# Two passes of a graph kernel on one core: narrower products of ones on TensorE in the last turns of both passes

## The chip, the core and the metric

One core of a Trainium2 chip runs the kernel. The metric is the device time of one execution in microseconds (us), lower is better. Engines are named as in the profile: PE is TensorE's matrix products, PEld its weight loads, DVE is VectorE, ACT is ScalarE, POOL is GpSimd, SP is SyncE, which here only issues transfers. A "q" behind an engine's name (SPq, ACTq) is its queue of issued transfers.

## What is computed

There are 100,000 nodes with 64 features each and 50,000 edges (src, dst) with 32 attributes each. Cut to what matters:

```python
h = relu(layernorm(x))                       # first layer
s, m, c = segment_sum(attr, src), segment_max(attr, src), count(src)
f = concat([s, m, s / max(c, 1), u[0]])      # 97 features of a node
x = x + relu(f @ W1 + b1) @ W2 + b2
h = relu(layernorm(x))                       # second layer
agg = segment_sum(h[src], dst)
x = x + relu(agg @ W.T + b)
```

The `h` of the first layer is not used by it. A node with no edge gets a constant row in either layer, a node with edges gets its own; so the work is done by edge, in sorted order, and the rows are then spread over the nodes.

## The kernel before

**Blocks and passes.** The edges are sorted by src first (up to about 226 us, not touched here). Then come two passes, each over 98 blocks (`BLOCKS`) of 512 edges (`BLK`). Pass 1 (side 0, about 226 to 730 us) computes the rows of the first layer and adds them to x, giving the table `node_table`. Pass 2 (side 1, about 731 us to the end) gathers rows of `node_table` for the source node of each edge, normalizes them, multiplies them by W, and adds the result to the table on the way to the output. Edge rows go out to memory as records (`records<-rec`, line 694), one store for a block. Of them, windows are loaded back: for each step of 1,024 nodes, eight windows of 112 records (`win<-records`). In pass 1 SP issues six of the eight (line 388) and ACT two (line 667); in pass 2 each issues four.

**Expansion.** The helper `expand(side, m)` on PE turns the windows of node step m into 1,024 node rows. Eight products (lines 1378 and 1379), each of a 128 by 128 one-hot matrix with 64 columns of a window, fill one bank of PSUM with 512 columns. In fp32 each product shows in the profile as two weight loads and two products, so an expansion is 16 records. What it needs: its one-hot matrices (`hot_ok`, made by DVE at line 1095: tile `oneh` in pass 1, `shared` in pass 2), and a free bank (`added`, counted by DVE after it has added a finished expansion to the table's rows, lines 1114, 1116 and, for the last twelve steps of pass 2, 1105). The banks are `p_t` and `p_u` in pass 1 and `p_t`, `p_u`, `p_z` in turn in pass 2.

**Products of ones.** The helper `stream(bank, width)` at line 1384 multiplies a matrix of ones with `width` columns of ones into a bank that the following expansion overwrites. Nothing reads the result. In `expand` it stands between the wait for the bank and the wait for the one-hots, over 512 columns (line 1376); this is the product ahead. In pass 2 a second one, over 256 columns, stands behind each expansion but the last (lines 1423 to 1425), with a wait for the next bank; this is the product behind. Each shows in the profile as two records of PE at line 1384.

**Order by hand.** Each engine runs a list of turns n, each turn working on blocks and steps of different age. In pass 1 PE does in turn n the transposes of block n+1, the expansion of step n-6 (`SRC_EXP`), the second layer of block n-1 (line 1367) and the first of block n (line 1360). Turns 98 to 103 have no new block. In pass 2 PE does in turn n the expansion of step n-9 (`DST_EXP`), the product behind, the multiplication by W of block n-2 (`conv`, line 1416) and the transposes of block n (`turn_h`, line 1408). Turns 98 to 106 have no new block: they expand steps 89 to 97, and the first two also have a `conv`. DVE in turn n of pass 2 reads the keys of windows n-8 (line 1085), takes the moments of block n, makes the one-hots of step n-8 (line 1095), normalizes block n (line 1182) and adds step n-10. SP and ACT load the windows of step n-6.

**Rings.** There are two buffers of one-hots: in pass 2 line 1093 makes the one-hots of step m wait until expansion m-2 is done. There are four buffers of windows: in pass 2 the loads for step m wait until expansion m-4 is done (lines 386 and 665), and until the records of block m+1 are stored. In pass 1 SP has the wait for the expansion only for the last step, ACT for the last six. ACT's queue also holds, ahead of its window loads in each turn, the copy of a block into a record and its store (lines 683 to 694). SP's queue holds, behind its window loads, the loads of the table's rows and the stores of finished ones (lines 394, 398, 424).

Of the kernel before, what the change touches and what calls it, by code (L numbers as in the profile page):

```python
# [26 lines left out]
BLK = BT * P  # L27
BLOCKS = -(-E // BLK)
# [32 lines left out]
SRC_REC, SRC_WIN, SRC_HOT, SRC_EXP, SRC_ADD, SRC_PUT = 1, 3, 5, 6, 7, 9  # L61
DST_TAKE, DST_CONV, DST_REC, DST_WIN, DST_HOT, DST_EXP, DST_ADD, DST_PUT = 1, 2, 3, 6, 8, 9, 10, 12
# [7 lines left out]
def valid(n):  # L70

    return 0 <= n < BLOCKS


def build(nc, x, src, dst, edge_attr, u, W1, b1, W2, b2, W, b, src_keys, dst_keys, src_cols, dst_cols, dst_lines, out):
# [5 lines left out]
    with ExitStack() as ctx:  # L81
# [258 lines left out]
        def _(sp):  # L340
# [35 lines left out]
            def windows(side, m):  # L376

                g = BLOCKS * side + m
                starts = start_row[side][0:1, PER * m:PER * m + SP_LOADS[side]]
                _, at = nc.values_load_multi_w_load_instructions(starts, engines=[mybir.EngineType.SP], min_val=0, max_val=E * ROW,  # L380
                                                                 skip_runtime_bounds_check_because="each start is a count of rows, lowered to its limit on the chip")
                for n in range(AHEAD + 1) if m == 0 else [min(m + AHEAD, BLOCKS - 1)]:
                    stored = BLOCKS * side + n
                    sp.wait_ge(rec_out[stored % RRING], 16 * (stored // RRING + 1))
                if side == 1 or m == BLOCKS - 1:
                    sp.wait_ge(expanded, g - WRING + 1)
                for q in range(SP_LOADS[side]):
                    sp.dma_start(win[g % WRING][0:WP, q, :].bitcast(U8), window_rows(side, at[q])).then_inc(win_in[g % WRING], 16)
# [220 lines left out]
        def _(act):  # L609
# [45 lines left out]
            def upper_windows(side, m):  # L655

                g = BLOCKS * side + m
                starts = start_row[side][0:1, PER * m + SP_LOADS[side]:PER * (m + 1)]
                _, at = nc.values_load_multi_w_load_instructions(starts, engines=[mybir.EngineType.Activation], min_val=0, max_val=E * ROW,
                                                                 skip_runtime_bounds_check_because="each start is a count of rows, lowered to its limit on the chip")  # L660
                for n in range(AHEAD + 1) if m == 0 else [min(m + AHEAD, BLOCKS - 1)]:
                    stored = BLOCKS * side + n
                    act.wait_ge(rec_out[stored % RRING], 16 * (stored // RRING + 1))
                if side == 1 and m < WRING or m >= BLOCKS - DST_WIN:
                    act.wait_ge(expanded, g - WRING + 1)
                for q in range(PER - SP_LOADS[side]):
                    s.dma_start(win[g % WRING][0:WP, SP_LOADS[side] + q, :].bitcast(U8), window_rows(side, at[q])).then_inc(win_in[g % WRING], 16)  # L667
# [615 lines left out]
        def _(pe):  # L1283
# [15 lines left out]
            def sum_starts(side, nth):  # L1299

                pe.wait_ge(s_above, nth)
                for h, row in enumerate(p_s[side]):
                    for k in range(SPAN):
                        last = mm(row[0:1, 0:400], in_group[:, k:k + 1], above[:, k, 400 * h:400 * (h + 1)],
                                  start=k == 0, stop=k == SPAN - 1)
                last.then_inc(s_base, 1)
# [43 lines left out]
            def turn_attr(n):  # L1350
                if n == 1:
                    pe.wait_ge(s_col, 2)
                pe.wait_ge(scaled, n + 1)
                for t in range(BT):
                    last = tr(p_g[n % 2][0:2 * FE, t::BT], xa[n % XRING][:, t, :], ident[:, :])
                last.then_inc(turned, 1)

            def layer1(n):
                pe.wait_ge(feats_ok, n + 1)
                mm(p_z[n % 2][:, :], w1_s[:, :], feats[n % 2][:, :], start=True, stop=True).then_inc(z_ok, 1)  # L1360

            def layer2(n):
                pe.wait_ge(hid_ok, n + 1)
                if n >= 1:
                    pe.wait_ge(copied, n)
                for t in range(BT):
                    last = mm(p_m[0][:, D * t:D * (t + 1)], hid[n % 2][:, P * t:P * (t + 1)], w2_s[:, :], start=True, stop=True)  # L1367
                last.then_inc(m_ok, 1)

            def expand(side, m):  # L1370
                k = BLOCKS * side + m
                ring = p_e[side]
                to = ring[m % len(ring)]
                if side == 1 or m >= 2:
                    pe.wait_ge(added, max(k - len(ring) + 1, BLOCKS * side))
                stream(to, BLK)
                pe.wait_ge(hot_ok, k + 1)
                for s in range(PER):
                    last = mm(to[:, D * s:D * (s + 1)], hots[side][m % HRING][:, s, :], win[k % WRING][:, s, 0:D], start=True, stop=True)  # L1379
                last.then_inc(expanded, 1)  # L1380

            def stream(bank, width):

                mm(bank[:, 0:width], one[:, :], one[:, :].unsqueeze(1).to_broadcast([P, width // P, P]), start=True, stop=True)  # L1384

            turn_attr(0)
            for n in range(BLOCKS + SRC_EXP):
                if valid(n + 1):
                    turn_attr(n + 1)
                if n == 2:  # L1390
                    sum_starts(0, 2)
                if valid(n - SRC_EXP):
                    expand(0, n - SRC_EXP)
                if valid(n - 1):
                    layer2(n - 1)
                if n == 15:
                    pe.wait_ge(s_wrong, 1)
                    mm(p_m[1][0:1, 0:1], wrong1[:, 0:1], one[:, 0:1], start=True, stop=True).then_inc(s_wsum, 1)
                if valid(n):
                    layer1(n)  # L1400

            pe.wait_ge(s_fast, 1)
            with pe.If(pe.value_load(fast[0:1, 0:1], min_val=0, max_val=1)):

                def turn_h(n):
                    pe.wait_ge(h_ok, n + 1)
                    for h in range(2):
                        last = tr(p_g[n % 2][:, P * h:P * (h + 1)], hn[n % 2][:, 2 * h:2 * h + 2, :].rearrange("p t d -> p (t d)"), ident[:, :])  # L1408
                    last.then_inc(ht_ok, 1)

                def conv(n):
                    k = BLOCKS + n
                    pe.wait_ge(hts_ok, n + 1)
                    pe.wait_ge(copied, max(k - 1, BLOCKS))
                    for h in range(2):
                        last = mm(p_d[1][n % 2][:, P * h:P * (h + 1)], agg[n % 2][:, P * h:P * (h + 1)], wd[:, :, :].rearrange("p t d -> p (t d)"),
                                  start=True, stop=True)
                    last.then_inc(m_ok, 1)

                for n in range(BLOCKS + DST_EXP):  # L1420
                    if valid(n - DST_EXP):
                        expand(1, n - DST_EXP)
                    if valid(n - DST_EXP) and valid(n - DST_EXP + 1):
                        pe.wait_ge(added, max(BLOCKS + n - DST_EXP + 1 - len(p_e[1]) + 1, BLOCKS))
                        stream(p_e[1][(n - DST_EXP + 1) % len(p_e[1])], BLK // 2)
                    if valid(n - DST_CONV):
                        conv(n - DST_CONV)
                    if valid(n):
                        turn_h(n)
# [61 lines left out]
```

## Time and profile before

| | |
|---|---|
| median of 3 runs | 1256.63 us |
| lowest and highest of them | 1252.74, 1262.65 us |
| the profiled execution's own time | 1261.67 us |
| its span, first to last instruction | 1259.8 us |
| mean granted clock of TensorE | 0.888 of 2.4 GHz |

The profile is of one execution, 5.0 us above the median of the three runs. A line of a timeline or of the chain gives a start and a length in us, the engine, the line of the kernel and the operation; in brackets stands how long the engine had been idle before it and what ended that. In a table of windows the granted clock (PEclk) is 1.00 at 2.4 GHz and 0.50 at 1.2 GHz.

### The profile page before, as it was taken

How to read it: one execution, taken by the hardware profiler on the slowest of the kernel's cores; microseconds unless marked ns; L12 is line 12 of the kernel's file. 1: busy time of each engine (PE TensorE's matmuls, PEld its weight loads, DVE VectorE, ACT ScalarE, POOL GpSimd, SP SyncE). 2: the span in 40 equal slices, each digit the busy share in tenths (PEclk: the TensorE clock that was granted, in tenths of full speed). 3: DMA queues.
4: the chain of work that ended last, by engine and by line, in shares of the span. 5: the costliest groups of instructions: out<-in, count | busy, mean ns of one | idle time of the engine just before them, and what ended most of it. 6: DMA issues, size and time to landing. Idle time of an engine off the chain costs nothing.

```text
span 1259.8 us, 20767 instructions
## 1 busy us (share of the span) xinstructions
PE 960.6 (76%) x5818; PEld 758.0 (60%) x5818; DVE 1030.1 (82%) x2727; ACT 280.1 (22%) x681; POOL 758.0 (60%) x821
## 2 busy tenths in 40 slices
PE   0131027979999999999999823879889788888888
PEld 0010014757777777777777613767767677677777
DVE  8888887899999999999999624777777777777774
ACT  1441042212222222222222101112112112111110
POOL 3000046667777777777776067777777777777750
PEclk9995556889999999999999955898999989988899
DMA  2000012767899888888888654777788778777775
GB/s 65 0 0 0 0 53 68 175 161 206 236 232 240 234 226 219 241 220 236 230 222 240 164 173 98 180 201 203 210 222 207 202 198 210 210 208 201 203 186 156
DMA packets 317563, 218.51 MB, mean 173 GB/s; under 512 B 223428, under 2 KB 255140, under 8 KB 317444
## 3 DMA queue, kind: packets, MB, share of 16 engines
q1 hardware_dynamic: 182100, 135.41, 38.7%
q10 hardware_dynamic: 110256, 62.42, 18.8%
q0 software_dynamic: 25088, 19.32, 8.6%
q8 instruction: 47, 0.77, 0.3%
q14 instruction: 72, 0.59, 0.1%
HBM read 137.51 MB, written 79.45 MB: 172 GB/s over the span
## 4 chain that ended last, share of the span: by engine, by line
DVE 36%; POOL 20%; DMA 13%; PE 11%; issue 10%; ACTq 5%; ACT 2%; SPq 0%; POOLq 0%; DVEq 0%
POOL xa L559 11%; POOL xa L540 9%; DMA xa<-node_table,gi 8%; DMA win<-records 5%; DVE feats L1074 4%; DVE feats L1072 4%; ACTq L667 3%; DVE oneh L1095 3%; DVE dout L1114 2%; PE p_m L1367 2%; DVE kb L920 2%; DVE ka L920 2%; DVE shared L1095 2%; DVE ka L921 2%; DVE kb L921 2%
## 5 line engine op out<-in xcount | busy, mean ns | idle before, releaser
L540 POOL DMA_INDIRECT xa<-in_edge_attr_dram,gi x392 | 375.2, 957 | 252.3 <-issue 115.4
L559 POOL DMA_INDIRECT xa<-node_table,gi x392 | 369.9, 944 | 158.7 <-issue 105.8
L677 ACT ACTIVATE hid<-p_z,bias_z 128x512 f32<-128x512 f32 x98 | 113.4, 1157 | 249.2 <-issue 230.0
L1408 PE MATMUL p_g<-ident,hn 128*128 128x128 f32 x196 | 46.6, 325 | 106.9 <-DVE hn L1182 106.5
L1074 DVE TENSOR_TENSOR_SCAN feats<-c_rows,feats,p_g 32x512 f32<-32x512 f32 x97 | 123.3, 1271 | 1.4
L1095 DVE SCALAR_TENSOR_TENSOR shared<-p_m,node_of 112x1024 f32<-112x1024 f32 x98 | 117.1, 1195 | 6.8 <-PE p_z L1379 3.4
L1072 DVE TENSOR_TENSOR_SCAN feats<-c_rows,feats,p_g 64x512 f32<-64x512 f32 x97 | 122.5, 1263 | 0.1
L1367 PE MATMUL p_m<-w_s,hid 128*128 128x64 f32 x784 | 109.3, 284 | 15.8 <-ACT hid L677 15.4
L730 ACT ACTIVATE sd<-mv,eps_t 128x4 f32<-128x4 f32 x98 | 29.1, 297 | 413.2 <-DVE mv L1173 350.4
L1095 DVE SCALAR_TENSOR_TENSOR oneh<-p_m,node_of 112x1024 f32<-112x1024 f32 x98 | 119.3, 1217 | 0.2
L1360 PE MATMUL p_z<-feats,w_s 96*128 96x512 f32 x196 | 112.4, 657 | 6.2 <-DVE feats L1074 6.2
L1168 DVE BATCH_NORM_STATS2 stat<-xa 128x6 f32<-128x64 f32 x392 | 58.7, 212 | 67.6 <-DMA xa<-node_table,gi 63.9
L1379 PEld LDWEIGHTS p_u<-win,oneh 128*128 128x128 f32 x784 | 97.1, 195 | 26.9 <-issue 22.5
L1384 PE MATMUL p_t<-one 128*128 128x256 f32 (+1 forms) x228 | 112.5, 578 | 0.0
L1379 PEld LDWEIGHTS p_t<-win,oneh 128*128 128x128 f32 x784 | 96.4, 194 | 25.5 <-issue 24.1
L1384 PE MATMUL p_u<-one 128*128 128x512 f32 x230 | 110.7, 566 | 0.0
L1367 PEld LDWEIGHTS p_m<-w_s,hid 128*128 128x128 f32 x784 | 97.6, 196 | 21.5 <-ACT hid L677 19.9
L1379 PE MATMUL p_u<-win,oneh 128*128 128x64 f32 x784 | 94.9, 275 | 2.2 <-DVE oneh L1095 2.2
L1408 PEld LDWEIGHTS p_g<-ident,hn 128*128 128x128 f32 x196 | 25.0, 159 | 117.8 <-DVE hn L1182 116.9
L1085 DVE COPY p_m<-win 112x8 f32<-112x8 f32 x196 | 32.8, 167 | 75.9 <-DMA win<-records 75.7
L1379 PE MATMUL p_t<-win,oneh 128*128 128x64 f32 x784 | 93.9, 273 | 0.5 <-DVE oneh L1095 0.5
L1182 DVE SCALAR_TENSOR_TENSOR hn<-xa,mv,p_m 128x64 f32<-128x64 f32 x392 | 83.9, 276 | 3.5
(253 smaller groups left out, 1539.3 us busy)
## 6 DMA issues: line engine op xcount, KB each, us to landing
win<-records SPq DMA_DIRECT2D x980, 28.9 KB
records<-rec ACTq DMA_DIRECT2D x196, 132.0 KB
din<-in_x_dram SPq DMA_DIRECT2D x49, 512.0 KB
node_table<-dout SPq DMA_DIRECT2D x49, 512.0 KB, 3.6
din<-node_table SPq DMA_DIRECT2D x43, 512.0 KB
out_dram<-dout SPq DMA_DIRECT2D x43, 512.0 KB
c_rows<-rows_src ACTq DMA_DIRECT2D x141, 128.0 KB
win<-records ACTq DMA_DIRECT2D x588, 28.9 KB
```

The costliest lines, as they stand in the source:

```text
L540: g.indirect_dma_start(out=xa[n % XRING][:, t, 0:FE], out_offset=None, in_=edge_attr, in_offset=bass.IndirectOffsetOnAxis(ap=gi[0][:, BT * ...
L559: g.indirect_dma_start(out=xa[k % XRING][:, t, :], out_offset=None, in_=T, in_offset=bass.IndirectOffsetOnAxis(ap=gi[1][:, BT * n + t:BT * ...
L677: s.activation(hid[n % 2][:, :].rearrange("p (t n) -> p n t", n=P), p_z[n % 2][:, :].rearrange("p (n t) -> p n t", t=BT), ACT.Relu, bias=b ...
L1072: v.tensor_tensor_scan(f[0:64, :], c[0:64, at:at + BLK], p_g[n % 2][0:64, :], first[0:64], ALU.mult, ALU.add)
L1074: v.tensor_tensor_scan(f[64:96, :], c[64:96, at:at + BLK], p_g[n % 2][0:32, :], first[64:96], ALU.min, ALU.max).then_inc(feats_ok, 1)
L1095: v.scalar_tensor_tensor(hots[side][m % HRING][0:WP, :, :], key_at(k).unsqueeze(2).to_broadcast([WP, PER, UNIT]), -float(STEP * m), node_o ...
L1182: last = v.scalar_tensor_tensor(hn[n % 2][:, t, :], xa[(BLOCKS + n) % XRING][:, t, :], mv[n % 2][:, t, 0:1], up[:, t:t + 1].to_broadcast([ ...
L1360: mm(p_z[n % 2][:, :], w1_s[:, :], feats[n % 2][:, :], start=True, stop=True).then_inc(z_ok, 1)
L1367: last = mm(p_m[0][:, D * t:D * (t + 1)], hid[n % 2][:, P * t:P * (t + 1)], w2_s[:, :], start=True, stop=True)
L1379: last = mm(to[:, D * s:D * (s + 1)], hots[side][m % HRING][:, s, :], win[k % WRING][:, s, 0:D], start=True, stop=True)
L1384: mm(bank[:, 0:width], one[:, :], one[:, :].unsqueeze(1).to_broadcast([P, width // P, P]), start=True, stop=True)
L1408: last = tr(p_g[n % 2][:, P * h:P * (h + 1)], hn[n % 2][:, 2 * h:2 * h + 2, :].rearrange("p t d -> p (t d)"), ident[:, :])
```

## The change

In turns that have no new block, the product ahead of an expansion covers 128 columns in place of 512, and in pass 2 the one behind it is left out, with its wait. In pass 1 this is so in turns 99 to 103 (steps 93 to 97; turn 98 keeps 512). In pass 2 it is so in turns 98 to 106 (steps 89 to 97); the product behind is issued in turns 9 to 97 and no longer in turns 98 to 105.

```diff
-            def expand(side, m):
+            def expand(side, m, ones=BLK):
...
-                stream(to, BLK)
+                stream(to, ones)
...
-                    expand(0, n - SRC_EXP)
+                    expand(0, n - SRC_EXP, BLK if n <= BLOCKS else BLK // 4)
...
-                        expand(1, n - DST_EXP)
-                    if valid(n - DST_EXP) and valid(n - DST_EXP + 1):
+                        expand(1, n - DST_EXP, BLK if valid(n) else BLK // 4)
+                    if valid(n - DST_EXP) and valid(n):
                         pe.wait_ge(added, max(BLOCKS + n - DST_EXP + 1 - len(p_e[1]) + 1, BLOCKS))
                         stream(p_e[1][(n - DST_EXP + 1) % len(p_e[1])], BLK // 2)
```

## Rows read from the trace of the kernel before

**Rows 1.** The page: busy time by engine, and the chain's shares

```profile
PE 960.6 (76%) x5818; PEld 758.0 (60%) x5818; DVE 1030.1 (82%) x2727; ACT 280.1 (22%) x681; POOL 758.0 (60%) x821
...
DVE 36%; POOL 20%; DMA 13%; PE 11%; issue 10%; ACTq 5%; ACT 2%; SPq 0%; POOLq 0%; DVEq 0%
```

**Rows 2.** Chain of waits, last turns of pass 2: start us, us, what

```profile
1225.72 0.67 PE p_g L1408 x2
1226.39 1.71 PE p_z L1384 x2
1228.10 2.32 PE p_z L1379 x16
1230.42 0.49 PE p_t L1384 x2
1230.91 0.44 PE p_m L1416 x4
1231.35 0.86 PE p_t L1384 x2
1232.21 1.73 PE p_t L1379 x16
...
1252.85 1.34 PE p_u L1384 x4
1254.19 1.75 PE p_u L1379 x16
```

**Rows 3.** Table of windows: length, busy of PE, PEld, DVE, ACT, POOL, PEclk, DMA, GB/s

```profile
1178.50:1188.20 9.70, 9.63 (x32) 7.39 (x32) 7.53 (x34) 1.96 (x8) 7.26 (x9) 0.50 0.75 199
...
1223.80:1225.70 1.90, 0.12 (x2) 0.00 (x0) 1.86 (x7) 0.73 (x4) 0.00 (x0) 1.00 0.32 55
1225.90:1229.20 3.30, 3.30 (x11) 2.27 (x11) 2.29 (x5) 0.74 (x3) 0.00 (x0) 0.50 0.42 102
1229.30:1255.90 26.60, 26.60 (x178) 22.25 (x177) 14.36 (x22) 0.93 (x4) 0.00 (x0) 1.00 0.61 169
708.00:720.00 12.00, 11.33 (x77) 8.72 (x75) 7.01 (x11) 1.48 (x2) 0.00 (x0) 1.00 0.59 146
...
724.00:727.00 3.00, 2.43 (x13) 2.24 (x11) 1.23 (x2) 0.00 (x0) 0.00 (x0) 0.51 1.01 391
```

**Rows 4.** Chain of waits, last turns of pass 1

```profile
720.05 1.79 DMA win<-records
...
722.07 1.23 DVE oneh L1095
...
723.35 3.09 PE p_u L1379 x16
726.46 0.70 DVE dout L1114
```

**Rows 5.** Chain of waits, a stretch of pass 2 at the low clock

```profile
1180.96 3.31 PE p_u L1379 x16
1184.27 0.96 PE p_z L1384 x2
1185.23 0.85 PE p_m L1416 x4
```

**Rows 6.** Timeline, last turns of pass 1, PE and DVE

```profile
718.37 2.00 PE L1379 MATMUL p_t<-win,oneh 128*128 128x64 f32 x16 [0.51 <-DVE oneh L1095]
...
724.86 0.69 DVE L1114 TENSOR_TENSOR dout<-p_t,din 128x512 f32<-128x512 f32 x1 [1.56 <-DMA din<-in_x_dram]
```

**Rows 7.** Timeline, last turns of pass 2, windows' loads and keys

```profile
1236.32 9.91 ACTq L667 DMA_DIRECT2D win<-records  x16
...
1240.68 1.73 SPq L388 DMA_DIRECT2D win<-records  x4
...
1246.82 0.17 DVE L1085 COPY p_m<-win 112x8 f32<-112x8 f32 x1 [1.34 <-DMA win<-records]
```

**Rows 8.** Table of windows, two us in which PE waited for DVE

```profile
1202.00:1204.00 2.00, 0.93 (x6) 0.51 (x5) 1.84 (x8) 0.06 (x1) 1.41 (x2) 1.00 0.94 335
```

## The prediction

> **What bounds the kernel now.** I read the page first, then the chain of waits at the end of either pass, then tables of windows with the granted clock, then the timeline. Over the whole span PE is busy for 960.6 us and has 11% of the chain; DVE has 36% [rows 1]. That mean says little here, since the change touches 14 of the 196 expansions, all of them where a pass runs out.
>
> At the end of pass 2 the picture is another one. From 1225.72 us, when the last transposes start, to 1255.94 us, when the last expansion is done, the chain is PE alone [rows 2], and from 1229.3 to 1255.9 PE is busy for all of 26.60 us, DVE for 14.36 [rows 3]. The reader should see the pattern of a turn: products of ones for 1.34 us (0.49 behind and 0.86 ahead), then an expansion for 1.73, together 3.08 us. So 44% of the path is work whose result nobody reads.
>
> At the end of pass 1 no product of ones is on the chain. It ends with a load of windows that lands at 721.84, one-hots until 723.30, the last expansion from 723.35, and DVE's add from 726.46 [rows 4].
>
> **The change in pass 2.** It removes 9 times 384 columns ahead and 8 products of 256 columns behind. By TensorE's granted clock, all of this costs one of two prices.
>
> At 2.4 GHz (PEclk 1.00): 512 columns take 0.86 us [rows 2], so 128 take 0.22, and the `conv` products confirm it: four records of 128 columns in 0.44 us. A turn's own PE work falls from 3.08 us to 0.22 + 1.73 + about 0.05 = 2.0 us.
>
> At 1.2 GHz (PEclk 0.50): an expansion takes 3.31 us, the product of 256 columns behind it 0.96, `conv` 0.85 [rows 5], and 512 columns take 1.71 [rows 2]. So 128 columns take 0.43. The first record behind an expansion costs 0.11 more (0.96 against half of 1.71). A turn is then 0.43 + 0.11 + 3.31 = 3.85 us, which is more than the 3.08 of today. An expansion at the low clock loses 1.58 us, and the removed products give back 1.12 at most at the high one (0.64 + 0.49). The sign hangs on which level the last nine turns get.
>
> What do the rows show of the level? PE stands idle from about 1223.9 to 1225.7, waiting for the last block's normalization, and the clock then is 0.50 from 1225.9 to 1229.2 [rows 3]. Today that low stretch is filled with the transposes, a product of 512 columns, and some of an expansion, and the clock is back at 1.00 from 1229.3. After the change only 128 columns stand there, and from then on nearly all of PE's time is expansions. The nearest rows to such a mix at the low level are from 1178.5 to 1188.2: PE busy for 9.63 of 9.70 us with an expansion, products of ones and `conv`, and the clock at 0.50 for all of it [rows 3]; it rose only as a `conv`, transposes and a whole product of 512 columns had followed each other. Expansions with their many weight loads did not bring it up there; 512 columns in a row did, there and at 1229. The change takes away just these. I therefore take the low price for all nine turns.
>
> The sum, from 1226.39 where the product ahead of step 89 starts: nine expansions, 9 x 3.31 = 29.79; the first product ahead, 0.43; two gaps with `conv`, each 0.96 + 0.43 = 1.39, so 2.78; six gaps of 0.54, so 3.24. Together 36.24 us, up to 1262.63. Today it is 29.55 us, up to 1255.94 [rows 2]. Pass 2 ends 6.7 us later.
>
> All else stays hidden: DVE needs 0.17 + 1.23 + 0.69 = 2.1 us a turn [rows 4, 6, 7], and the windows' loads need less than four turns of 3.85 (below). The wait that goes with the product behind is for a bank that the next expansion waits for anyway, so it costs and gives nothing; between 0 and 0.05 us a turn.
>
> In sentences of its own, the Trainium skill: the page "TensorE: Matmul & The Clock Gate", section "Why this matters for your kernels", says that keeping TensorE continuously busy brings it to full clock. By that rule the tail, in which products still follow each other without a gap, would be back at 1.00 soon after 1229, and the result would be that of the third case below. This trace doesn't bear it out: 9.63 us busy of 9.70, at 0.50 throughout [rows 3].
>
> **The change in pass 1.** It removes 5 times 384 columns, 5 x 0.64 = 3.2 us of PE's time at the high clock, from a stretch in which PE is busy for 11.33 of 12.00 us [rows 3] but in which the last expansions wait for one-hots: step 96 starts at 718.37, released by DVE after an idle 0.51 us [rows 6], and step 97 is released by DVE at 723.35. Nothing of the gain is on the path: 0. What can be lost is the clock. If it falls before 720, step 96 takes 3.31 and a wait of about 0.4 behind step 95 instead of 2.0, and ends near 722.2. Its add by DVE waits for a load until 724.86 anyway [rows 6], and step 97's one-hots don't wait for it. Step 97 takes 3.09 now, most of it at the low level (0.51 from 724.0 [rows 3]); wholly at the low level it takes 3.31. So pass 1 costs +0.2 us; bounds: 0 and, if each of five expansions were on the path at 1.58 us more, 7.9. I take 0.2, since the chain's order (load, one-hots, expansion) doesn't lead through earlier expansions.
>
> Both parts: +6.9 us. On the profiled execution's own time, 1261.67 (span 1259.8 and 1.9 around it), that makes 1268.6. That execution is 5.0 above the median of the three runs, so on the median, 1256.6, I forecast 1263.5 us.
>
> **The rivals.** *Upper level at first, then lower.* Idle time does not always bring the clock down: from 1202 to 1204 PE was busy for only 0.93 of 2.00 us and the clock stayed 1.00 [rows 8]. So in some executions step 89 starts at 1.00. Then PE has 2.0 us of work a turn and must wait for windows: the load of step 96's windows may start when expansion 92 is done at 1240.54; SP starts it at 1240.68, it has landed at 1246.82 [rows 7], and 0.28 later, with 1.23 for the one-hots and 1.75 for the expansion, the ring of four is closed: 9.5 us for four steps, 2.4 us a turn, and ACT's 9.91 us for 16 loads say 2.5. PE idles a fifth of each turn, more in the first ones, where ACT still has copies and stores ahead of its loads, and the clock may fall midway. Four turns at 2.4 save 4 x 0.68 = 2.7, five at 3.85 lose 3.8: together with pass 1 +1.3, 1258 us.
>
> *Upper level all the way.* Then eight turns of 2.4 to 2.5 us, 19.6, follow on step 89's end, which comes at about 1228.4. The end is 1248.0 instead of 1255.94; with the ACT queue's first turns about 7 us are gained: 1250 us. For it speaks that PE at 1.95 of 2.4 us is busier than in 1202 to 1204; against it, the idle stretch of 1223.9 to 1225.7 with so little behind it.
>
> *Slower beyond what can be told.* The clock falls in pass 1's last turns as well, and there the expansions become the path. It decides from the point where an expansion at the low level with its product, 3.85 us, is longer than the time between one-hots, 3.4 to 5 us now (718.37 to 723.35). Then up to 7.9 us come on top: 1271 us. Against it speaks the wait of 0.51 us that is there to be used, and that loads set the last step.
>
> That the change doesn't do what it says I exclude: each narrower product is certain to be issued as written.
>
> **How the numbers follow.** Forecast (low level in pass 2's tail, 1263.5): 0.57. Mixed (1258): 0.22. Upper level throughout (1250): 0.13. Pass 1 on the path too (1271): 0.06. The rest, 0.02, is for a gain in which even the ring of windows is faster. Runs of the kernel before spread by 5 us to either side, so each case has some 3 us of its own for a median. The forecast's own range is 1259 to 1268; the range takes in the mixed case down to twice its spread, 1258 - 6 = 1252, and on the other side a part of pass 1's bound, 1263.5 + 6.5 = 1270; the case at 1250 is mostly left out. A measurement of this kernel can tell about 1%, 12.6 us, from no change. No case but the last one reaches it, and part of the forecast's upper end: slower 0.08. Faster by it would need more than the ring of windows gives: 0.02. Within 1%: 0.90.
>
> **What would show it.** Right: in pass 2's tail PE without gaps, PEclk 0.50 from about 1226 to the end, expansions of 3.31 us, turns of 3.85; the last add near 1262.6 of the same start; pass 1's end later by no more than 0.4. Wrong: PEclk 1.00 behind 1230 with keys (line 1085) waiting for the windows' loads in every turn, turns of 2.4 us; or PE waiting at line 1379 for one-hots; or in pass 1 step 97's expansion released by PE's own queue and not by DVE.

## The result and the profile after

| | before | changed |
|---|---|---|
| median | 1257.90 us (20 runs) | 1263.47 us (20 runs) |
| lowest and highest | 1252.74, 1269.87 | 1257.20, 1274.43 |
| the profiled execution | 1261.67 | 1257.20 |
| mean granted clock in it | 0.888 | 0.873 |

The changed kernel takes 1.0037 times the time of the one before (95% interval 1.0021 to 1.0054). On 1257.9 us that is 4.7 us more, between 2.6 and 6.8. The loss is below the 1% of the forecast's bound, but with 20 runs a side it is clear of the noise. The three runs shown ahead of the prediction had a median of 1256.63, the twenty have 1257.90.

The profiled execution of the changed kernel was its fastest of twenty. Whole spans therefore can't be compared, nor the shares of the chain. They moved a great deal by themselves: DVE 36% and POOL 20% before [rows 1], and now

```profile
DVE 29%; POOL 25%; PE 15%; DMA 12%; issue 11%; ACTq 5%; ACT 2%; DVEq 0%; POOLq 0%; SPq 0%
```

Nor do PE's 15%, after 11%, come from the two ends of the passes that the change touches: there expansions and products of ones have some 30 us of the chain after the change, and some 33 before. DVE and POOL changed places in the middle of the passes, where the code is the same. What can be compared is a *tail*, from one instruction to another at the end of a pass. I use two. The tail of pass 2 goes from the start of the last transposes (line 1408) to the start of DVE's last add (line 1105): 1225.72 to 1255.96, 30.24 us, in the profile before. The tail of pass 1 goes from the start of the last block's second layer (line 1367) to the start of the last add (line 1114): 707.48 to 726.46, 18.98 us.

After the change, the timeline of PE and DVE in the last turns of pass 2, with the idle time before an instruction in brackets:

```profile
1221.39 0.44 PE L1408 MATMUL p_g<-ident,hn 128*128 128x128 f32 x2 [1.45 <-DVE hn L1182]
...
1221.89 1.90 PE L1379 MATMUL p_z<-win,shared 128*128 128x64 f32 x16
...
1229.77 2.00 PE L1379 MATMUL p_z<-win,shared 128*128 128x64 f32 x16 [0.79 <-DVE shared L1095]
...
1231.18 0.17 DVE L1085 COPY p_m<-win 112x8 f32<-112x8 f32 x1 [0.88 <-DMA win<-records]
...
1232.74 3.60 PE L1379 MATMUL p_t<-win,shared 128*128 128x64 f32 x16 [0.70 <-DVE shared L1095]
```

its chain of waits from there,

```profile
1232.74 3.60 PE p_t L1379 x16
1236.34 0.53 PE p_u L1384 x2
1236.88 3.31 PE p_u L1379 x16
...
1248.40 3.32 PE p_u L1379 x16
...
1251.74 0.69 DVE sign_out L1105
```

and a table of windows, with the busy time of PE, PEld, DVE, ACT and POOL, then the granted clock:

```profile
1219.70:1221.30 1.60, 0.24 (x3) 0.05 (x1) 1.56 (x7) 0.51 (x3) 0.00 (x0) 1.00 0.27 54
1221.40:1232.80 11.40, 9.91 (x85) 9.53 (x85) 7.95 (x13) 1.67 (x7) 0.00 (x0) 1.00 0.70 176
1233.00:1251.70 18.70, 18.70 (x88) 18.51 (x87) 8.96 (x14) 0.00 (x0) 0.00 (x0) 0.50 0.52 151
698.00:710.50 12.50, 9.62 (x71) 8.14 (x69) 6.82 (x12) 2.61 (x4) 0.00 (x0) 1.00 0.79 208
710.70:722.40 11.70, 11.36 (x52) 11.17 (x52) 4.95 (x8) 0.01 (x1) 0.00 (x0) 0.50 0.62 170
```

The reader should see a tail in two parts. Up to 1232.8 the clock is 1.00 and PE has time to spare: 9.91 us busy of 11.40, with steps 92 and 93 waiting for windows' keys and the one-hots made of them. From about 1233 the clock is 0.50, PE is busy without a gap, and a turn takes 0.53 + 3.31 = 3.84 us where it was 3.08 [rows 2]. What four steps gain at 2.4 GHz, five at 1.2 GHz lose: the tail is 1221.39 to 1251.74, 30.35 us against 30.24. In pass 1 the chain after the change reads

```profile
709.74 1.23 DVE oneh L1095
710.98 0.04 issue
711.02 3.68 PE p_u L1379 x16
714.70 0.53 PE p_t L1384 x2
715.23 3.31 PE p_t L1379 x16
718.54 0.53 PE p_u L1384 x2
719.07 3.32 PE p_u L1379 x16
722.41 0.70 DVE dout L1114
```

where before it went through a load and step 97's one-hots [rows 4]. The last three expansions run at the low level one behind the other and are the path; the first of them started late, after PE had waited 3.00 us for its one-hots. The tail is 702.18 to 722.41, 20.23 us against 18.98.

### The profile page after: what moved, and what is told of

The parts are those of the page before. It is cut to its first block, busy times and chain, and to the rows that moved or that the text cites. A ratio compares the mean times of both kernels' runs of the same rounds, so it can differ in the third digit from the quotient of the medians.

```text
span 1255.4 us, 20735 instructions
## 1 busy us (share of the span) xinstructions
PE 964.8 (77%) x5802; PEld 771.3 (61%) x5802; DVE 1031.4 (82%) x2727; ACT 280.5 (22%) x681; POOL 757.6 (60%) x821
## 4 chain that ended last, share of the span: by engine, by line
DVE 29%; POOL 25%; PE 15%; DMA 12%; issue 11%; ACTq 5%; ACT 2%; DVEq 0%; POOLq 0%; SPq 0%
POOL xa L540 15%; POOL xa L559 9%; DMA xa<-node_table,gi 8%; DMA win<-records 4%; ACTq L667 3%; PE p_u L1379 3%; PE p_t L1379 3%; DVE feats L1074 3%; DVE feats L1072 2%; DVE kb L920 2%; DVE ka L920 2%; DVE oneh L1095 2%; PE p_m L1367 2%; DVE shared L1095 2%; DVE ka L921 2%
## 5 line engine op out<-in xcount | busy, mean ns | idle before, releaser
L1384 PE MATMUL p_u<-one 128*128 128x512 f32 (+1 forms) x224 | 110.0, 576 | 0.0
L1384 PE MATMUL p_t<-one 128*128 128x256 f32 (+2 forms) x222 | 108.9, 575 | 0.0
L1379 PEld LDWEIGHTS p_t<-win,shared 128*128 128x128 f32 x528 | 79.1, 230 | 18.9 <-issue 17.2
```

## The experiments

Diffs are against the kernel before, unless said, and cut to the lines that matter: where a call has a width, `expand` and `stream(to, ones)` are as in the change. All of them change only products of ones, which nothing reads, and the waits that go with them. Each kernel was profiled once, so a tail is one execution's and says nothing of how often it comes; each was timed 8 to 12 times beside the kernel before on the same chip. The last column is the granted clock of TensorE over the whole kernel, as the mean of these timed executions, and behind the slash the same for the kernel before beside them. One execution's clock scatters by some 0.0045 around the mean, so a mean of twelve is good to about 0.0013. For the change itself it is the mean of its twenty.

| run | ratio to before, 95% | tail, pass 1 | tail, pass 2 | PE idle before the last transposes | clock in the tail of pass 2 | clock, all timed executions |
|---|---|---|---|---|---|---|
| before | 1 | 18.98 | 30.24 | 1.81 | low for 3.4 us, then high | 0.886 to 0.889 |
| the change | 1.0037, 1.0021 to 1.0054 | 20.23 | 30.35 | 1.45 | high, low from step 93 | 0.874 / not on record |
| pass 1's part | 1.0009, 0.9984 to 1.0033 | 19.31 | 28.57 | 0 | high | 0.883 / 0.888 |
| pass 2's part | 1.0020, 0.9993 to 1.0047 | 16.91 | 36.43 | 2.04 | low from step 89 | 0.878 / 0.888 |
| behind left out | 0.9991, 0.9960 to 1.0022 | 17.06 | 26.37 | 0.82 | high | 0.886 / 0.888 |
| 128 ahead, 256 behind | 0.9998, 0.9971 to 1.0025 | 17.77 | 28.92 | 1.54 | low 3.4 us, high, low at the end | 0.884 / 0.888 |
| the change again | 1.0018, 0.9989 to 1.0047 | 18.16 | 30.86 | 0.35 | high, low within step 92 | 0.873 / 0.886 |
| turn 98 full | 1.0007, 0.9979 to 1.0035 | 20.13 | 30.84 | 0 | high, low within step 93 | 0.875 / 0.886 |
| no products | 1.0006, 0.9976 to 1.0036 | 19.29 | 32.48 | 2.05 | low from step 89 | 0.876 / 0.886 |
| 256 ahead | 1.0019, 0.9990 to 1.0047 | 18.34 | 30.43 | 1.91 | low 10 us, high, low at the end | 0.881 / 0.886 |
| change, turn 97 filled | 1.0034, 1.0013 to 1.0054 | 20.02 | 29.61 | 0 | high, low within step 93 | 0.874 / 0.887 |
| behind out, turn 97 filled | 0.9978, 0.9957 to 1.0000 | 16.80 | 25.88 | 0 | high | 0.887 / 0.887 |
| behind left out, again | 0.9976, 0.9953 to 0.9999 | 19.22 | 26.67 | 0.94 | high | 0.886 / 0.887 |
| behind out, filled, again | 1.0005, 0.9980 to 1.0029 | 18.00 | 25.21 | 0 | high | 0.888 / 0.889 |

The last column tells what one profile each cannot: over all timed executions the clock is lower by 0.013 with the change (its second timing), by 0.005 with pass 1's part and by 0.010 with pass 2's part, and in the four timings that keep 512 columns ahead and leave out only the product behind it differs from the kernel before by some 0.001 or less, which is noise.

**Pass 1's part alone.**

```diff
-                    expand(0, n - SRC_EXP)
+                    expand(0, n - SRC_EXP, BLK if n <= BLOCKS else BLK // 4)
```

> Only pass 1's part of the change: 128 columns ahead of steps 93 to 97, pass 2 as before. Theory (pass 1's last step is set by its windows' loads, the products of ones are beside the path, and the expansions at the low clock cost a little): +0.2 to +1.5 us against the kernel before. Rival (the five expansions become the path at 3.31 in place of 1.73 us): +6 to +8 us. Second rival (the removed 3.2 us of products were on the path): -1 to -3 us.

The ratio says +1.1 us, with an interval from 2.0 less to 4.2 more. That leaves out the 6 to 8 us of the first rival. It does not leave out the second rival's -1 to -3 us; against that one speaks the profile, in whose chain of the last turns no product of ones stands. The chain still ends in the windows' load and the one-hots, but the last expansion runs at 1.2 GHz for all of its length:

```profile
719.15 1.78 DMA win<-records
...
721.17 1.24 DVE oneh L1095
...
722.45 3.69 PE p_u L1379 x16
726.16 0.70 DVE dout L1114
```

Over all profiles the tail of pass 1 has a mean of 19.6 us in the five with the narrow products (18.2 to 20.2) and of 18.0 us in the nine with 512 columns (16.8 to 19.3). The ranges overlap; the means differ by 1.5 us. The low level is not the narrow products' alone: it came in the last steps of all five tails with them, but also in four of the nine with 512 columns (the profile before, no products in pass 2, and the second timings of the two kernels with nothing behind), where PE had waited 1.27 to 2.16 us for one-hots and an expansion took up to 3.68 us.

**Pass 2's part alone.**

```diff
-                        expand(1, n - DST_EXP)
-                    if valid(n - DST_EXP) and valid(n - DST_EXP + 1):
+                        expand(1, n - DST_EXP, BLK if valid(n) else BLK // 4)
+                    if valid(n - DST_EXP) and valid(n):
```

> Only pass 2's part: 128 columns ahead of steps 89 to 97 and nothing behind steps 89 to 96. Theory (the clock of the tail decides): executions differ. With the low level from step 89 on +6.7 us, with the high level for the first half about +0 to +1.5 us; median +4 to +6 us; expansions of 3.31 us at the end of the profile. Rival (pass 2's part gains as its work at 2.4 GHz says, and pass 1 is what makes the change slower): -6 to -8 us.

This execution shows the forecast's case from end to end. The table of windows:

```profile
1226.00:1228.10 2.10, 0.14 (x2) 0.00 (x0) 2.06 (x8) 0.93 (x4) 0.00 (x0) 1.00 0.34 54
1228.80:1264.50 35.70, 35.70 (x169) 35.58 (x167) 16.04 (x25) 1.68 (x7) 0.00 (x0) 0.50 0.47 133
```

and the chain of waits:

```profile
1228.84 3.31 PE p_z L1379 x16
1232.14 0.96 PE p_m L1416 x4
1233.10 0.43 PE p_t L1384 x2
1233.53 3.31 PE p_t L1379 x16
...
1241.53 0.53 PE p_z L1384 x2
1242.06 3.31 PE p_z L1379 x16
...
1264.61 0.69 DVE sign_out L1105
```

PE is busy for 35.70 of 35.70 us, and for all of them at 1.2 GHz: expansions of 3.31 us, gaps of 1.39 with `conv` and of 0.53 without. From the first product ahead at 1228.62 to the last expansion's end it is 35.96 us; the forecast's sum said 36.24. The tail of 36.43 us is 6.2 longer than that of the profile before. The rival, that pass 2 gains and pass 1 loses, falls: the twelve timed executions give +2.5 us, between -0.9 and +5.9. That is also less than the +4 to +6 that I expected of them; by the medians, 1264.48 against 1260.11, it is 4.4. The profiled execution, 1270.10 us, is the second longest of the twelve and not the typical one.

**The product behind left out, alone.** Run twice.

```diff
-                    if valid(n - DST_EXP) and valid(n - DST_EXP + 1):
+                    if valid(n - DST_EXP) and valid(n):
```

> Only the product behind is left out in turns 98 to 105; the one ahead keeps its 512 columns in both passes. Theory (the product ahead alone holds the clock up once it is up, as it does in pass 1, where there is none behind): turns of 0.86 + 0.05 + 1.73 = 2.65 us in place of 3.08, eight of them, -3 to -4 us. Rival (any product taken out of the tail brings the low clock): a turn is 1.71 + 0.11 + 3.31 = 5.1 us, up to +16 us.

> The run with only the product behind left out once more, for a second profiled execution and more times: tail of pass 2 26 to 29 us (28 if the level falls in turn 97 and 512 columns bring it back), level high in the last eight turns; total -1 to -4 us against the kernel before. Rival (the first profile was lucky, the level falls midway in others): a tail over 31 us.

Half of the change's idea is sound. With 512 columns ahead of each expansion the clock stays up, and the work that is taken out comes off the tail:

```profile
1225.00:1252.00 27.00, 25.65 (x172) 20.31 (x172) 17.71 (x30) 1.67 (x7) 0.00 (x0) 1.00 0.64 174
```

The tails are 26.37 and 26.67 us, against 30.24 and 28.57 in the two profiles that have before's pass 2. The last steps wait for windows' keys instead. The rival (any product taken out brings the low clock) falls. The totals moved by 1.1 us the first time, less than the 3 to 4 expected and within the noise, and by 3.0 us the second.

**128 ahead, 256 behind.**

```diff
-                        expand(1, n - DST_EXP)
+                        expand(1, n - DST_EXP, BLK if valid(n) else BLK // 4)
```

> Pass 2 only: 128 columns ahead of steps 89 to 97, the 256 behind kept. Columns of ones in a turn: 384, against 768 before, 128 in the change and 512 in the run with the behind left out. Theory (fewer columns in the tail leave the clock low after PE's wait in turn 97, and 384 are between): at the high level 2.45 us a turn, -4 to -5 us; at the low level 0.96 + 0.43 + 3.31 = 4.7 us a turn, +14 us; I expect the median between -4 and +4 us, with more spread than before. Rival (it is a wait for the bank that goes with the product behind, not the clock, that matters): same sign and size as the run with the behind left out, mirrored.

The low level was entered behind the wait in turn 97, 2.1 us after the last transposes had started, left 3.4 us later, and entered again at 1247.2, in time for the last two steps. Tail 28.92 us, ratio 0.9998: between the change and the run without the product behind, as the theory has it. The wait for the bank is still there in this kernel and makes no difference that can be seen: at the high level a turn takes 2.44 us (1232.47 to 1234.91), and its products alone ask for 0.22 + 1.73 + 0.49.

**The change again, and with a full turn 98.** The first is the change's code with one empty line less, so its lines are one lower. The second, against the changed kernel:

```diff
-                        expand(1, n - DST_EXP, BLK if valid(n) else BLK // 4)
+                        expand(1, n - DST_EXP, BLK if n <= BLOCKS else BLK // 4)
```

> The change itself once more, for another profiled execution. Tail of pass 2 = from the start of the last transposes to DVE's last add; 30.2 us in the profile before, 30.4 in the first one after, 36.3 in that of pass 2's part alone. Theory (the granted clock decides each execution's tail): the tail is near 36 us if the level is low from step 89 on, 30 to 34 if it falls later, and each expansion in it takes either 1.7 or 3.3 us. Rival (the windows' loads decide it): tails alike, 29 to 31 us, whatever the level. Pass 1, from the last block's second layer to the last add: 19.5 to 21 us against 17 to 19 before.

> The change, but turn 98 keeps its 512 columns ahead of step 89 (nothing behind it). Theory: where the level falls in turn 97, the 512 columns can bring it back, and then it falls later or not at all; tail of pass 2 29 to 33 us, never 36. Rival (the low level is entered again whatever stands in turn 98, for the eight turns with 128 columns are too thin): 35 to 36.5 us in this profile too.

The change's second profile was like the first: high until 1240.1, then low for 21.7 us, tail 30.86 us. It lay within both expectations, so the level and not the tail's length is what speaks here: its expansions take 1.7 us up to 1239 and 3.3 after. Its tail of pass 1, 18.16 us, was shorter than the 19.5 to 21 that I expected. The run with the full turn 98 is inconclusive on its question. Its last transposes started without a wait, the level did not fall there, and the 512 columns had nothing to bring back; the level fell at 1246.5, after PE had waited 1.80 us for one-hots. The run with 256 columns ahead, below, keeps 512 in turn 98 too and does answer it.

**No products of ones in the tail of pass 2.**

```diff
-                stream(to, BLK)
+                if ones:
+                    stream(to, ones)
...
-                        expand(1, n - DST_EXP)
-                    if valid(n - DST_EXP) and valid(n - DST_EXP + 1):
+                        expand(1, n - DST_EXP, BLK if valid(n) else 0)
+                    if valid(n - DST_EXP) and valid(n):
```

> Pass 2 only: no product of ones at all in turns 98 to 106; pass 1 as before. Theory: nothing is left that could lift the level, so all but perhaps the first steps run at 1.2 GHz, but a turn is then the bare expansion, 16 x 0.2133 = 3.41 us, and the two conv at 0.85: from the last transposes 0.4 + 9 x 3.4 + 1.7 = 32.9 us to the last expansion's end, so a tail near 33 us, +2.5 to +3 us against before and 3 to 4 less than the change at the low level. Rival (the products of ones cost nothing by themselves, and the windows' loads or DVE set the tail): 30 us or less. Second rival (the 128 columns of the change are of use to the clock): longer than the change's 36.

```profile
1231.20:1262.80 31.60, 31.60 (x149) 31.48 (x148) 16.18 (x24) 1.68 (x7) 0.00 (x0) 0.50 0.54 150
```

The tail is 32.48 us, 0.5 below the sum. Both rivals fall: at the low level the 128 columns of the change only cost, 36.43 - 32.48, some 3.9 us for nine of them.

**256 ahead, nothing behind.**

```diff
-                        expand(1, n - DST_EXP)
+                        expand(1, n - DST_EXP, BLK if n <= BLOCKS else BLK // 2)
```

with `ones` as in the change and the product behind left out.

> A candidate: pass 1 as before; pass 2 with nothing behind in turns 98 to 105, 512 columns ahead in turn 98 and 256 in turns 99 to 106. Theory: at the high level PE needs 0.43 + 0.05 + 1.73 = 2.2 us a turn and waits for the windows' loads, 2.4 to 3 us a turn; tail 25 to 28 us, -3 to -4 us, if the level holds; in some executions it falls midway, and each step after it costs 0.96 + 3.31 = 4.3 us. Against the run with 512 ahead and nothing behind (26.4 us from the last transposes) I expect a gain of 0 to 1 us or a loss. Rival (the fewer columns of ones the shorter the tail, the clock is by the way): 24 us or less in any execution.

```profile
1229.20:1239.30 10.10, 10.10 (x46) 9.74 (x45) 5.21 (x9) 1.68 (x7) 0.00 (x0) 0.50 0.41 101
1239.50:1252.90 13.40, 12.33 (x100) 11.58 (x100) 7.82 (x11) 0.00 (x0) 0.00 (x0) 1.00 0.71 189
1253.10:1258.20 5.10, 5.06 (x22) 4.49 (x21) 2.43 (x5) 0.00 (x0) 0.00 (x0) 0.50 0.55 206
```

A miss: 30.43 us where I expected 25 to 28. The level fell at about 1229.1, behind turn 97's wait of 1.91 us, stayed low for 10.2 us, came back while a `conv` and 256 columns stood next to each other, and fell again before the last step. This is no candidate.

Its timeline also shows what 512 columns in turn 98 do and do not:

```profile
1227.77 0.44 PE L1408 MATMUL p_g<-ident,hn 128*128 128x128 f32 x2 [1.91 <-DVE hn L1182]
1228.05 1.02 PE L1384 MATMUL p_z<-one 128*128 128x512 f32 x2
1228.91 3.29 PE L1379 MATMUL p_z<-win,shared 128*128 128x64 f32 x16
1231.99 1.17 PE L1416 MATMUL p_m<-wd,agg 128*128 128x128 f32 x4
1232.95 1.06 PE L1384 MATMUL p_t<-one 128*128 128x256 f32 x2
```

The 512 columns behind the wait still ran at the high level, and they neither kept it nor brought it back; nor did the first `conv` with 256 columns next to it, from 1231.99. Only the second such pair, from 1237.11, did.

**The wait in turn 97 filled.** Added to the change, and to the kernel with nothing behind (this one twice):

```diff
+                    if n == BLOCKS - 1:
+                        for _ in range(2):
+                            stream(p_e[1][(n - DST_EXP + 1) % len(p_e[1])], BLK)
                     if valid(n):
                         turn_h(n)
```

> The change, with PE's wait in turn 97 filled: two products of 512 columns of ones into the next bank ahead of the last transposes, 1.71 us at 2.4 GHz. Theory: the low level of the worst executions comes from that wait, so step 89 starts at the high level in every execution, and the level falls later, in turns with 128 columns that wait for windows; tail of pass 2 (last transposes to last add) 29 to 32 us, not 36; total about 2 us below the change. Rival (where the level falls has nothing to do with the wait): a tail of 36 us is as likely as without the filling, or the level is low in step 89.

> Candidate: the kernel before with nothing behind in turns 98 to 105, 512 columns ahead as before, and the wait in turn 97 filled with two products of 512 columns. Theory: high level from turn 97 to the end in every execution, turns of 2.65 us, tail of 25 to 27 us against 28.6 to 30.2 before: -2 to -4 us in all. Rival (the two added products delay the last transposes and the turns behind): the transposes start later by up to 1.7 us and the gain is gone, -1 to +1 us.

> The candidate (nothing behind in turns 98 to 105, 512 columns ahead, the wait in turn 97 filled) once more. Theory: tail of pass 2 25 to 27 us with all nine expansions at 1.7 us, total -3 to -4 us against the kernel before, ratio 0.997 to 0.998. Rival (the first time was chance, the totals differ by less): ratio 0.999 to 1.001, or a tail over 28 us with some expansions at 3.3.

In all three profiles step 89 runs at the high level, as the theory wants. But only one of them had a wait to fill. In the first profile with nothing behind, PE came to the filling at 1221.31, and DVE's rows were ready at 1222.90. In the other two PE was late anyway: it came at 1230.29 with the rows ready since 1228.6, and at 1224.31 with the rows ready since 1222.4. So these two say nothing of whether the wait lowers the level. In the change the high level doesn't last: the level is 0.50 from 1244.0 on, the tail 29.61 us, and the total (1.0034) is no better than the change's, not the 2 us that I had put down. The timeline of that run shows what the filling costs when PE is late:

```profile
1230.29 1.88 PE L1384 MATMUL p_z<-one 128*128 128x512 f32 x4
1232.00 0.38 PE L1408 MATMUL p_g<-ident,hn 128*128 128x128 f32 x2
```

and in the same run's timeline of DVE

```profile
1227.75 0.86 DVE L1182 SCALAR_TENSOR_TENSOR hn<-xa,mv,p_m 128x64 f32<-128x64 f32 x4
```

DVE's rows had been ready since 1228.6, so the 1.7 us of filling delayed the last transposes by 1.7 us. With nothing behind and the wait filled, the tails are 25.88 and 25.21 us, all nine expansions at the high level. A tail starts at the last transposes, so it leaves out what the filling costs: some 0.1 us in the first of these profiles and 1.7 in the second, which makes it 26.9. But the totals of the two times differ: 0.9978 (0.9957 to 1.0000) and 1.0005 (0.9980 to 1.0029). The second lies where the rival had put it. Without the filling they were 0.9991 and 0.9976. In the profiles the tail is shorter by some 3 us; over the four comparisons the mean ratio is 0.9988, 1.5 us less, with two intervals that hold 1, one that ends at it and one that ends just below. That the kernel before is beaten is likely and not settled. Nothing shows that the filling helps. Against the change's 1.0037 the mean is 0.5% less, against the 1.0028 that the change has as the mean of its two timings 0.4%.

## Why the prediction was right, and where not

**The sign and the mechanism: right.** The forecast was that the granted clock of the tail, and not the columns removed, decides; the measured time of 1263.47 us is the 1263.5 of the forecast. That the digits agree is luck. The forecast was 6.9 us above the median of before; measured by the ratio it is 4.7, by the medians 5.6, and before's median itself came out 1.3 higher with more runs. The term of pass 2 was too large and that of pass 1 too small, and the three errors cancelled.

**What bounds pass 2's end: right.** PE alone, with 44% of the path in products of ones. Taking some of them out shortened it to 26 us where the level stayed high.

**The price at the low level: right.** Expansion 3.31, gaps 1.39 and 0.54 forecast; 3.31, 1.39 and 0.53 measured; 36.24 us forecast for the stretch and 35.96 measured, in the one profile that was low from step 89 on.

**"I therefore take the low price for all nine turns": right only for some executions.** This was the step that mattered and it was too sure. It put pass 2 at +6.7 us; pass 2's part timed by itself gives +2.5, between -0.9 and +5.9. The changed kernel's own profile carries two of the three signs that I had named for being wrong: PE waiting at line 1379 for one-hots, for 0.79 and 0.70 us, and in pass 1 the last expansion started by PE's own queue. Of three profiles with the changed pass 2, one was low from step 89 on (36.43 us), and two were what I had as the mixed rival, the first with four steps at 2.4 GHz and five at 1.2 GHz (30.35), the second with three and six (30.86). I had given the first 0.57 and the second 0.22. The four steps at 2.4 GHz also took longer than the mixed rival's 2.4 us a turn: 10.85 us from step 89 to step 93, 2.7 a turn. Which case an execution gets goes with PE's wait ahead of the last transposes. There are eleven profiles without the filling. In the five where PE had been idle for 1.54 us or more (1.54, 1.81, 1.91, 2.04, 2.05), the level was low within 2.2 us of the last transposes' start; in the six with 1.45 or less (1.45, 0.94, 0.82, 0.35 and twice next to nothing) it stayed high there. That wait depends on how late the last gather lands and how late PE itself is; the one profile of before had 1.81, and I read it as the rule. I had also read from [rows 3] that 512 columns in a row bring the level back; the run with 256 columns ahead had 512 right behind the wait and stayed low for 10.2 us, so that reading doesn't hold as a rule.

How often an execution starts low isn't measured; it was one of the three profiles with the changed pass 2, and five of the eleven. With half of the executions starting low, the tail of pass 2 would be (36.4 + 30.6) / 2 = 33.5 us against (30.2 + 28.6) / 2 = 29.4 before: an estimate of +4.1 from these profiles. With 1.5 for pass 1 it gives 5.6, between the ratio's 4.7 and its upper end of 6.8. With one in three it gives 4.6.

**Pass 1, "+0.2 us": mis-sized.** Two things went wrong in it. I took the last expansion's 3.09 us at the kernel before [rows 4] as its usual length, though it took only 1.9 to 2.2 us in seven of the nine profiles with this code; and I held that the path doesn't lead through earlier expansions. In the profile after the change it does, for three of them. The measured term is 1.1 us with an interval that reaches from -2.0 to +4.2, and 1.5 us as a difference of mean tails. The direction is not clear of the noise in the time of this part alone; that the clock falls is, by 0.005 over twelve executions, as forecast.

**The ring of windows: right as a bound.** Where the level stayed high, the last steps waited for windows' keys, and no tail was below 25.2 us.

**The rule of the Trainium skill.** The page "TensorE: Matmul & The Clock Gate", section "Why this matters for your kernels", says that continuous work brings TensorE to full clock. These traces don't agree. In the run of pass 2's part PE was busy for 35.70 of 35.70 us at 0.50, in the run without products for 31.60 of 31.60. The measurement decides: with these small products, nearly each with a weight load of its own, continuous work was not enough here. The case that the rule gave (1250 us, 0.13) was seen in no profile of the change.

What stays open: that the low level costs what the sum says is shown; what sets it off is not. No experiment made the wait in turn 97 longer on purpose, so that its idle time governs the level is read from the order of eleven profiles, whose longest wait without a fall (1.45 us) and shortest with one (1.54) lie close together, and from the one profile in which the filling took a wait away. In pass 1 PE waited 2.00 and 2.16 us in two tails with 512 columns ahead and the expansion behind it still took 2.0 and 2.1 us, so the length of the last wait is not all of it. Why the clock came back in the run with 256 columns ahead and not in the one with 128 was not tried by itself either.

## What to carry to other kernels

Work that only holds the clock up has two prices, and the sum must be made at both: here a turn went from 3.08 us to 2.0 on paper and, wherever the level was low, to 3.84 in fact, since each expansion then took 3.31 us in place of 1.73. Take such work out where enough of it stays next to the real products (nothing behind, 512 columns ahead: the level held in pass 2's tail in four profiles of four, though in pass 1's tail, with 512 columns ahead too, it fell in four of nine) and not where PE has just had a wait, since behind the longer waits it fell. And when a change's worth hangs on a state that one profile shows once, look at a second profile, or at other places of the same trace where the wait was shorter, before calling it the rule. The mean granted clock of all timed executions helps too: it shows whether the level changed in more than the one execution that was profiled.

## What was not expected

- The high level is lost in the tail also without a long wait. In the change's first profile it fell near 1233, when PE had waited 0.79 and 0.70 us in two turns, at 9.91 us busy of 11.40.
- A PE that is late at one place and early at the same place in the next execution: the last transposes waited between 0 and 2.05 us for DVE in fourteen profiles, and in two of those with the filling they came over 3 us after their rows were ready, 1.7 of them by the filling itself (1228.6 and 1232.0 in the one shown). Filling a wait that is not always there costs its length when it isn't.
- The spread of a pass's tail with the same code is as large as the change's effect: pass 1's tail with 512 columns is 16.8 to 19.3 us in nine profiles.
